# A gating stage in which the projection's bias moves into TensorE's sums, the rows to send get a third buffer, and ScalarE writes the normalised rows

## The reference

```
x = layernorm(x + attention(x))            # attention ends in  y @ W_proj + b_proj
logits = tokens @ gate_w.T                 # 8 experts
expert = argmax(softmax(logits))           # the best expert of each token, with its probability
rank   = how many earlier tokens chose the same expert
keep   = rank < capacity                   # capacity is 640 tokens per expert
h   = relu(tokens @ w1[expert] + b1[expert])
ans = probability * (h @ w2[expert] + b2[expert])   # 0 for a token over capacity
x = layernorm(x + ans)
```

## Time and profile before

| | |
|---|---|
| time, median of 3 runs | 1352.88 us (1350.56 to 1355.76) |
| the profiled execution | 1350.51 us, its span 1348.6 us |
| mean granted TensorE clock over the span | 0.945 |
| the gating part | from about 958 us to 1084 us of the span |

### The profile page before, as it was taken

How to read it: one execution, slowest core, us unless ns; L and a number is a source line. 1 busy time by engine, 2 the same in 40 slices (tenths; PEclk the granted TensorE clock), 3 DMA queues, 4 the chain that set the end, 5 groups by cost and what they waited for, 6 DMA issues and landing times. The chain is left out here.

```text
span 1348.6 us, 22141 instructions
## 1 busy us (share of the span) xinstructions
PE 1239.5 (92%) x7669; PEld 618.8 (46%) x7669; DVE 1130.6 (84%) x2612; ACT 772.6 (57%) x1082; POOL 278.6 (21%) x382
## 2 busy tenths in 40 slices
PE   7997999999999999999999999999677469999996
PEld 4552233333333333333333333332366369999996
DVE  7989999999999999999999999992488548888886
ACT  3541267667667667667667667668344444454452
POOL 3344011111111111111111111111444501111221
PEclk9996699999999999999999999999877679999998
DMA  5694342302302202302302300121356223333330
GB/s 181 180 210 118 49 47 53 85 12 53 85 11 53 87 9 53 91 5 53 91 5 53 89 7 30 45 68 56 102 149 212 106 85 120 116 108 106 101 111 18
DMA packets 99471, 108.34 MB, mean 80 GB/s; under 512 B 18588, under 2 KB 88095, under 8 KB 99360
## 3 DMA queue, kind: packets, MB, share of 16 engines
q1 hardware_dynamic: 95776, 98.46, 27.4%
q0 software_dynamic: 3584, 8.47, 1.8%
HBM read 72.60 MB, written 40.26 MB: 84 GB/s over the span
## 5 line engine op out<-in xcount | busy, mean ns | idle before, releaser
L612 ACT ACTIVATE probs<-scores 128x1024 f32<-128x1024 f32 (+3 forms) x640 | 539.0, 895 | 290.7 <-PE scores L453 290.2
L715 DVE TENSOR_REDUCE part_max<-ring 128x1 f32<-128x512 f32 x768 | 477.9, 683 | 23.5 <-PE ring L493 23.1
L493 PE MATMUL ring<-k_stack,q_stack 96*128 96x512 bf16 (+3 forms) x1280 | 400.6, 362 | 10.6 <-ACT v_s L582 4.9
L453 PE MATMUL scores<-q_stack,k_stack 99*128 99x512 bf16 (+3 forms) x1280 | 338.6, 349 | 8.3 <-DMA q_stack<-max_rows 5.7
L473 PE MATMUL out_p<-probs,v_s 128*17 128x512 f32 (+3 forms) x2560 | 295.7, 534 | 0.5 <-POOL probs L782 0.3
L493 PEld LDWEIGHTS ring<-k_stack,q_stack 96*128 96x128 bf16 x1280 | 114.0, 97 | 308.4 <-DVE part_max L715 146.1
L709 DVE CUSTOM_DVE_ANT_0 scratch<-ring,mask_s 128x384 f32<-128x384 f32 (+2 forms) x384 | 196.5, 554 | 32.1 <-PE ring L493 29.0
L453 PEld LDWEIGHTS scores<-q_stack,k_stack 99*128 99x128 bf16 x1280 | 112.6, 98 | 182.6 <-issue 57.0
L782 POOL TENSOR_SCALAR_AFFINE_SELECT probs<-probs 128x512 f32<-128x512 f32 x128 | 81.2, 635 | 396.5 <-ACT probs L612 380.5
L1383 PE MATMUL psY<-w_hi,h_hi 128*128 128x256 f32 x320 | 90.9, 284 | 0.0
L1417 ACT ACTIVATE h_whole<-psH,b_s 128x384 f32<-128x384 f32 (+1 forms) x128 | 66.9, 528 | 41.5 <-PE psH L1364 33.7
(11 more groups left out here) (116 smaller groups left out, 1378.0 us busy)
## 6 DMA issues: line engine op xcount, KB each, us to landing
w_whole<-w SPq DMA_DIRECT2D x16, 1024.0 KB, 6.3
q_stack<-pieces_d SPq DMA_DIRECT2D x192, 64.0 KB, 2.9
k_stack<-pieces_d SPq DMA_DIRECT2D x168, 64.0 KB, 3.1
o_d<-o_s SPq DMA_DIRECT2D x32, 256.0 KB, 2.3
slots_d<-no_row SPq DMA_DIRECT2D x8, 650.0 KB, 6.1
xe<-slots_d SPq DMA_DIRECT2D x8, 650.0 KB
xin<-x SPq DMA_DIRECT2D x8, 512.0 KB, 5.0
pieces_d<-hi SPq DMA_DIRECT2D x32, 128.0 KB, 3.4
```

Of the source, the lines that this page charges most:

```text
L453: last = nc.tensor.matmul(scores[p][:, hh, off:CHUNK], k_stack[i][0:KROWS, kb // TPC, j, kb % TPC * P:(kb % TPC + 1) * P], q_stack[i][0:KR ...
L493: last = nc.tensor.matmul(slot[:, h * w:(h + 1) * w], q_stack[i][0:SROWS, qt // TPC, j + h, qt % TPC * P:(qt % TPC + 1) * P], k_stack[i][0 ...
L612: nc.scalar.activation(probs[n % NPROB][:, 2 * p:2 * p + 2, off:CHUNK], scores[p][:, :, off:CHUNK], ACT.Exp, scale=SCALE).then_inc(exp_don ...
L715: nc.vector.tensor_reduce(part_max[:, qt, j, t:t + 1], ring[m % 3][:, 0:w], axis=AX.X, op=ALU.max).then_inc(ring_read, 1)
```

## The change

Three edits, all in `project_and_gate`.

1. GpSimd's `add_bias` and its buffer `xb` are gone. For each tile `project` begins with a matmul of one row of ones (`ones_f`, one partition) with the first row of `bias_s`, which starts the sum in `psC[t]`; the two old matmuls add to it. These 4 matmuls stand ahead of the wait for `yT`. TensorE waits once, at the start of the part, for the bias itself. VectorE's `residual` adds `x_s` instead of `xb`, and SyncE's load of the next x into that buffer waits for the residual of the chunk instead of the addition on GpSimd.
2. `rows` and `slot_index` have three buffers (`NROWS`) instead of two.
3. The 4 instructions on VectorE that wrote the normalised rows are gone. VectorE computes a `shift` per token (minus mean times reciprocal deviation, one small scalar_tensor_tensor), and ScalarE writes the rows in `norm_rows` with a scale and a bias per token.

```diff
-            def add_bias(n, i, h):
-
-                pool.wait_ge(loaded[i], 48 * (h + 1))
-                if not (isinstance(n, int) and n == 0):
-
-                    pool.wait_ge(res_ready, 1 + TPC * (n - 1))
-                nc.gpsimd.tensor_tensor(xb[i][:], x_s[i][:], bias_s[:].unsqueeze(1).to_broadcast([P, TPC, C]),
-                                        ALU.add).then_inc(xb_ready, 1)
...
             def project(n):
-                pe.wait_ge(yT_ready, n + 1)
                 for t in range(TPC):
                     if n:
                         pe.wait_ge(res_ready, 1 + TPC * (n - 1) + t + 1)
+                    nc.tensor.matmul(psC[t][:, 0:C], ones_f[:], bias_s[0:1, :], start=True, stop=False)
+                pe.wait_ge(yT_ready, n + 1)
+                for t in range(TPC):
                     for kt in range(KT):
                         last = nc.tensor.matmul(psC[t][:, 0:C], yT[n % 2][:, kt, t * P:(t + 1) * P], wproj_s[:, kt, :],
-                                                start=(kt == 0), stop=(kt == KT - 1))
+                                                start=False, stop=(kt == KT - 1))
                     last.then_inc(projected, 1)
...
+            pe.wait_ge(bias_ready, 1)
+            pe.wait_ge(set_up, 3 + NROWS)
             project(0)
             project(1)
...
+            def norm_rows(n, i):
+                act.wait_ge(shift_ready, n + 1)
+                act.wait_ge(rows_sent[n % NROWS], 16 + 16 * TPC * (n // NROWS))
+                if n >= NROWS:
+                    act.wait_ge(plain_ready, 1 + TPC * (n - NROWS + 1))
+                for t in range(TPC):
+                    nc.scalar.activation(rows[n % NROWS][:, t, 0:C], res[i][:, t, :], ACT.Identity, scale=rstd[i][:, t:t + 1],
+                                         bias=shift[i][:, t:t + 1]).then_inc(rows_ready, 1)
...
                 exponentials(n)
+                if n + 1 < NC3:
+                    norm_rows(n + 1, 1 - n % 2)
                 plain_rows(n, n % 2, n // 2, range(TPC))
...
-                nc.vector.tensor_tensor(res[i][:, t, :], psC[t][:, 0:C], xb[i][:, t, :],
+                nc.vector.tensor_tensor(res[i][:, t, :], psC[t][:, 0:C], x_s[i][:, t, :],
                                         ALU.add).then_inc(res_ready, 1)
...
-                for t in range(TPC):
-                    nc.vector.tensor_scalar(rows[i][:, t, 0:C], res[i][:, t, :], mv[i][:, t, 0:1],
-                                            rstd[i][:, t:t + 1], ALU.subtract, ALU.mult).then_inc(rows_ready, 1)
+                nc.vector.scalar_tensor_tensor(shift[i][:], mv[i][:, :, 0], -1.0, rstd[i][:],
+                                               ALU.mult, ALU.mult).then_inc(shift_ready, 1)
...
-                sp.wait_ge(xb_ready, n + 1)
+                sp.wait_ge(res_ready, 1 + TPC * (n + 1))
                 sp.dma_start(x_s[i][:], gate_srcs["x"][n + 2]).then_inc(loaded[i], 16)
```

More of the change, by code:

```diff
@@ L802 @@
 NOWHERE = 1.0e6
+NROWS = 3
 TILES = B * T // P
@@ L828, in project_and_gate @@
         eps_s = sb("eps_s", [P, 1])
-        primer = sb("p3_primer", [2, P])
+        primer = sb("p3_primer", [NROWS, P])
         count_s = sb("count_s", [P, E])
-        xb = [sb(f"xb{i}", [P, TPC, C]) for i in range(2)]
+        ones_f = sb("ones_f", [1, P])
         yT = [sb(f"yT{i}", [P, KT, CHUNK]) for i in range(2)]
@@ L841, in project_and_gate @@
         rstd2 = [sb(f"rstd2_{i}", [P, TPC]) for i in range(2)]
-        rows = [sb(f"rows{i}", [P, TPC, RW]) for i in range(2)]
+        shift = [sb(f"shift{i}", [P, TPC]) for i in range(2)]
+        rows = [sb(f"rows{i}", [P, TPC, RW]) for i in range(NROWS)]
         plain = [sb(f"plain{i}", [P, TPC, C]) for i in range(2)]
@@ L858, in project_and_gate @@
         slot1 = sb("slot1", [P, TPC])
-        slot = [sb(f"slot_index{i}", [P, TPC], U32) for i in range(2)]
+        slot = [sb(f"slot_index{i}", [P, TPC], U32) for i in range(NROWS)]
         psC = [ps(f"psC{t}", [P, CHUNK]) for t in range(TPC)]
@@ L894, in project_and_gate @@
         slots_ready = sem("slots_ready")
-        rows_sent = [sem(f"rows_sent{i}") for i in range(2)]
+        rows_sent = [sem(f"rows_sent{i}") for i in range(NROWS)]
         NC3 = B * NCH
@@ L973, in turn_x1 @@
                         last = nc.tensor.transpose(psD[:, kt, t * P:(t + 1) * P],
-                                                   rows[i][:, t, kt * P:(kt + 1) * P], id_s[:])
+                                                   rows[n % NROWS][:, t, kt * P:(kt + 1) * P], id_s[:])
                 last.then_inc(x1_turned, 1)
@@ L1036, in plain_rows @@
                     act.wait_ge(rstd2_ready, n + 1)
+                    act.wait_ge(rows_ready, TPC * (n + 1))
                     act.wait_ge(plain_stored[i], 1 + 16 * h)
                 for t in tiles:
-                    nc.scalar.activation(plain[i][:, t, :], rows[i][:, t, 0:C], ACT.Copy,
+                    nc.scalar.activation(plain[i][:, t, :], rows[n % NROWS][:, t, 0:C], ACT.Copy,
                                          scale=rstd2[i][:, t:t + 1]).then_inc(plain_ready, 1)
             first_root(0, 0)
+            norm_rows(0, 0)
             for n in range(NC3):
@@ L1055, in _ @@
             nc.vector.memset(count_s[:], 0.0).then_inc(set_up, 1)
-            for i in range(2):
+            for i in range(NROWS):
                 nc.vector.memset(rows[i][:, :, C:RW], 0.0).then_inc(set_up, 1)
-            dve.wait_ge(set_up, 4)
+            nc.vector.memset(ones_f[:], 1.0).then_inc(set_up, 1)
+            dve.wait_ge(set_up, 3 + NROWS)
             dve.wait_ge(w_loaded, 16 * (n_w - 1))
@@ L1077, in residual @@
                 dve.wait_ge(projected, m + 1)
-                if t == 0:
-                    dve.wait_ge(xb_ready, n + 1)
-                nc.vector.tensor_tensor(res[i][:, t, :], psC[t][:, 0:C], xb[i][:, t, :],
+                if t == 0 and n >= 2:
+                    dve.wait_ge(rows_ready, TPC * (n - 1))
+                nc.vector.tensor_tensor(res[i][:, t, :], psC[t][:, 0:C], x_s[i][:, t, :],
                                         ALU.add).then_inc(res_ready, 1)
@@ L1132, in choose, with place @@
                 nc.vector.tensor_tensor(onehot[:], wanted[:], per_tile(best[:]), ALU.is_equal).then_inc(onehot_ready, 1)
-            def place(n, i):
+            def place(n):
                 dve.wait_ge(onehot_ready, n + 1)
@@ L1142, in place @@
                 wait_step(n, 5)
-                step(n, 7, nc.vector.reciprocal(rows[i][:, :, PROB], total[:]))
+                step(n, 7, nc.vector.reciprocal(rows[n % NROWS][:, :, PROB], total[:]))
                 dve.wait_ge(ranks_ready, n + 1)
@@ L1146, in place @@
                                                    ALU.add))
-                step(n, 9, nc.vector.tensor_copy(rows[i][:, :, TOKEN], token_s[:]))
+                step(n, 9, nc.vector.tensor_copy(rows[n % NROWS][:, :, TOKEN], token_s[:]))
                 wait_step(n, 8)
@@ L1174, in _ @@
                 choose(n - 1)
-                norm_chunk(n, i, n // 2)
-                place(n - 1, 1 - i)
+                norm_chunk(n, i)
+                place(n - 1)
             norm_plain(NC3 - 1, 1)
             choose(NC3 - 1)
-            place(NC3 - 1, 1)
+            place(NC3 - 1)
         @block.gpsimd
         def _(pool):
-            for i in range(2):
+            for i in range(NROWS):
                 nc.gpsimd.dma_start(primer[i:i + 1, :], ident[i:i + 1, :]).then_inc(rows_sent[i], 16)
@@ L1186, in _, with send @@
             pool.wait_ge(w_loaded, 16 * (n_w - 1))
[L1187 to L1198 removed]
+            def send(n):
                 done = in_register(pool, 1 + (n + 1))
@@ L1203, in send @@
                     nc.gpsimd.indirect_dma_start(
[L1204 to L1218, removed]
+                        slots_d, bass.IndirectOffsetOnAxis(ap=slot[n % NROWS][:, t:t + 1], axis=0),
+                        rows[n % NROWS][:, t, :], None, bounds_check=E * CAP - 1, oob_is_err=False,
+                    ).then_inc(rows_sent[n % NROWS], 16)
+            for n in range(NC3):
+                send(n)
+            for i in range(NROWS):
+                pool.wait_ge(rows_sent[i], 16 + 16 * TPC * len(range(i, NC3, NROWS)))
 def experts(nc, slots_d, w_whole, w1, b1, w2, b2, ident, out_d):
```

18 lines of the change are left out of this document (7 added, 11 removed).

## The result

The changed kernel takes 1358.11 us (median of 20 runs, 1353.49 to 1362.2) against 1353.41 (20 runs, 1350.36 to 1359.25). The ratio is 1.0027, with a 95% interval of 1.0016 to 1.0039: slower by 0.3%. That is within the half per cent that I had called no change, but outside the forecast's range, and the interval leaves out 1. The profiled execution's span is 1353.7 us, and its mean granted clock over the span is 0.945, as before.

What follows compares the result with a forecast made beforehand. The prediction took the loop residual, `yT`, projection, rank matmuls, `place` as the bound. Five chunks -12.6, start -1.0 and end -0.9 sum to -14.5 us, from 1352.88 to 1338.5 us; range 1333 to 1350 for 8 in 10.

Steps and rivals of the forecast that it cites:

- What bounds the kernel: Gating chunks: the loop through TensorE's projection sets 13.4 us per chunk; VectorE's work beside the projection has 0.93 us to spare.
- Four bias matmuls: TensorE, between logits and projection: at most 1.65 us per chunk at 2.4 GHz or 3.3 at 1.2, hidden in the gap.
- What they do to the clock: Ahead of the projection: idle gap shrinks from 2.61 to about 0.9 us, clock mostly holds, five chunks save 12.6 us.
- The first rival: Projection: the clock falls as before, chunks stay near 13.4 us, no change, 1351 us; chance 20%.
- The allowance of half a microsecond: Per chunk, for clock falls in the wait for `x1T` and the logits: 10.8 us instead of 10.3.
- The part's start: Start of gating: slow bias matmuls against earlier residuals, between -3 and +3 us, taken as -1 us.
- The part's end: After place(5), where no projection follows: ScalarE's rows end earlier than VectorE's did, -0.9 us.
- The late x: SyncE's load of the next x lands after `normalise` needs it, each chunk losing the difference; chance 2%.
- The slower rival: TensorE's list between logits and projection: bias at 1.2 GHz delays the projection 2.4 us per chunk, +12, 1365 us; chance 8%.

Runs made afterwards that it cites:

- e5: Changed kernel with the bias edit undone (GpSimd adds the bias again), three buffers and ScalarE's rows kept: 1354.42 us, ratio 1.0015.
- e1: Changed kernel with the bias matmuls on all 128 partitions, identity times the whole bias tile: 1340.73 us, ratio 0.9893.
- e2: Changed kernel with bias matmuls on 128 partitions of weights, 127 of them holding zeros: 1349.09 us, a single run.
- e8: e1 plus two full matmuls into a spare bank, between transposes and logits of each chunk with a projection behind it: 1340.04 us, ratio 0.9885.
- e7: Kernel before the change with four full matmuls per chunk put ahead of the projection, their sums overwritten: 1355.78 us, ratio 1.0018.
- e9: e1 with two buffers of rows instead of three: 1355.51 us, ratio 1.0013.
- e10: e1 unchanged, measured again: 1348.12 us, ratio 0.9941.
- e4: Changed kernel with the one-partition bias matmul closing each tile's sum in chunks 0 and 1 instead of opening it: 1368.09 us, ratio 1.0122.

## Why the prediction was wrong, point by point

- **What bounds the kernel** was right: the loop through residual, `yT`, projection, rank matmuls and `place`. VectorE gave up 3.9 us of busy time per chunk, as worked out, and the chunk didn't move; the wait before `rank_all` grew to 5.00 us where 4.8 was forecast. `wanted` fell to 0.19 us in the chunks and was back at 2.86 with the addition on GpSimd (e5), so its wait belongs to the addition. The row before shows only the common end, 997.20 and 997.14; `wanted` starts 0.42 us ahead of the addition.
- **Four bias matmuls**: 1.99 us per chunk where 1.65 was taken as the upper price, hidden as forecast.
- **The step that failed is "What they do to the clock".** It read "shrinks to about 0.9 us, with four full-width matmuls ahead of it", and took 256 columns for full work; on it rested a projection of 3.3 us and -12.6 us for the five chunks, where 5.1 to 6.8 us and -0.64 were measured. The matmuls were full in columns and had one partition of 128. The runs show in its place that behind such matmuls, and behind those with 32 or 64 partitions, the projection runs at 0.50 for most of its length (5.1 to 6.8 us in the changed kernel), and behind the same matmuls with 128 it doesn't (3.6 to 4.6 us in e1), zeros included (e2). What full ones do in e1 is bring the clock back sooner after its fall. That they would have kept it from falling in the changed kernel's list, with the copy wait left empty, no run shows, and e1 speaks against it. The first rival named this and got 20%; it should have had more, since no row of the trace showed such a matmul at either level. Its time, 1351, was missed too, by the start.
- **The allowance of half a microsecond** for copy wait and logits was too small in its own right. With full matmuls (e1) these still bring the clock down in every chunk, and a chunk takes 11.2 or 12.9 us, 0.9 or 2.6 above 10.3; only with the copy wait filled too (e8) is it 10.58.
- **The part's start**: forecast between -3 and +3 with -1 taken, measured +5.07. The larger piece is the one that the prediction named and didn't count in its -1: the bias of chunk 2 ran at 0.50 and held its projection up by 3.71 us, where 3 was the warning. The smaller is one that the range left out, the clock's rise being put off: the first projection ran at 0.54, and chunk 0's transposes came 2.4 us late, of which the logits gave 1.4 back. With full matmuls the start takes 28.9 to 30.2 us, 29.72 before.
- **The part's end**: -0.9 forecast, -0.58 measured between place(5) and place(7). ScalarE's rows take 2.07 us, not the 1.69 of the nearest row: they are 0.50 us apart and not 0.40. Whether that is the whole difference no run shows.
- **The late x** didn't occur: no wait of VectorE on `yT` is to be seen in the chunks. **The slower rival** came half true in two places, with the bias of chunk 2 (above) and in the last chunk with a projection, where the bias took 3.43 us, most of it at 0.50.
- The sum of what was measured: +5.07 at the start, -0.64 in five chunks, -0.58 and -0.04 at the end, +3.81 us; the medians differ by 4.7.

## What to carry to other kernels

When a matrix engine's work between two waits looks slow, read the granted clock of that stretch before counting the work around it, and ask of every matmul meant to keep it up how many partitions it uses: here a bias added as one row of ones cost the time of a full matmul and did nothing for the clock. Fold such a term in with all partitions (the identity times the bias tile), which gives the same sum in the same columns. Then look for the second bound before rating an edit: here VectorE's room was worth nothing without the clock (the changed kernel), the clock nothing without the room (e7), and both nothing without the third buffer (e9). Together they gave 0.6 and 1.1% in two measurements (e10, e1).

## What the runs showed that I had not expected

- One-partition matmuls kept the clock at 0.50 through 27 us in which TensorE was busy almost without a gap (e4), though about two thirds of that time were full matmuls. The clock's rule for mixed work stays open beyond these cases.
- 127 partitions of zeros serve as well as data: 11.21 and 12.87 us per chunk in both.
- At the full clock a bias matmul with one partition costs no less than one with 128: 1.99 us for four (changed kernel) and 1.97 (e8).
